# A gated cross-attention block on one core: the first two batches in another order, and part of the ternary weights on GpSimd

## What is computed

```python
x = x + tanh(g_xattn) * attention(layernorm(x), ctx, ctx)
x = x + tanh(g_ffn) * ffn(layernorm(x))

def attention(query, key, value):
    qk = einsum('bhqd,bhkd->bhqk', Q, K)               # Q, K, V: 512x512 linear layers with bias
    scores = qk / sqrt(32)
    feats = [scores.mean(), scores.max(-1).mean(), var(softmax(scores)).mean()]   # per batch and head
    t = exp(clip(mlp(feats), log 0.1, log 10))
    return linear(softmax(qk / (2 * t)) @ V, Wo, bo)

def ffn(x):                                            # 512 -> 2048 -> 512
    return bitlinear(gelu(bitlinear(x, w1)), w2)

def quant_weight(w):                                   # inside bitlinear
    s = clip(mean(abs(w)), 1e-5, None)
    return clip(round(w / s), -1, 1) * s               # ternary
```

## Time and profile before

| | us |
|---|---|
| median of 3 runs | 1429.16 (1427.7 to 1429.87) |
| profiled execution | 1428.32 |
| its span | 1426.5 |
| busy in the span: TensorE (matmul) | 1208.2 (85%) |
| VectorE | 1124.8 (79%) |
| ScalarE | 921.8 (65%) |
| GpSimd | 396.9 (28%) |
| mean granted TensorE clock, of full speed | 0.933 |

### The profile page before, as it was taken

The page is one execution under the profiler, slowest core; times in us unless marked ns, Lnnn a source line. Parts: engine busy times, 40 slices in busy tenths (PEclk is TensorE's granted clock), DMA queues, the critical chain, the costliest instruction groups (busy, mean ns, idle before and its releaser), DMA issues.

```text
span 1426.5 us, 23442 instructions
## 1 busy us (share of the span) xinstructions
PE 1208.2 (85%) x6684; PEld 445.5 (31%) x6684; DVE 1124.8 (79%) x2057; ACT 921.8 (65%) x1527; POOL 396.9 (28%) x369
## 2 busy tenths in 40 slices
PE   3624678998999999998999899999989899869958
PEld 1200231144313442244314341244214331223224
DVE  7189966988698878988698869988798879993246
ACT  2445458956597549856795649855895669645803
POOL 5354412531155102531145104520253101100210
PEclk9755688999999999999999999999999999889979
DMA  8241113011210122012301121012302110001000
GB/s 313 74 148 45 23 40 101 16 45 45 84 37 21 27 69 83 16 45 46 104 16 45 33 65 55 16 46 53 97 16 46 45 60 1 1 0 60 1 0 30
DMA packets 35315, 73.70 MB, mean 52 GB/s; under 512 B 7792, under 2 KB 7792, under 8 KB 34672
## 3 DMA queue, kind: packets, MB, share of 16 engines
q1 hardware_dynamic: 35184, 72.10, 17.6%
HBM read 38.39 MB, written 8.39 MB: 33 GB/s over the span
## 4 chain that ended last, share of the span: by engine, by line
PE 51%; DVE 26%; ACT 10%; issue 9%; POOL 2%; DVEq 1%; DMA 1%; SPq 1%; ACTq 1%; POOLq 0%
PE b_ps L1193 11%; DVE stat L868 7%; ACT region L712 5%; PE o_ps L1375 5%; PE o_ps L1193 5%; DVE nmax L863 5%; PE z_ps L1193 5%; PE a_ps L1214 4%; PE o_ps L1233 4%; PE b_ps L1220 3%; ACT etile L695 3%; PE b_ps L1354 2%; PE z_ps L1375 2%; PE b_ps L1365 2%; PE z_ps L1244 2%
## 5 line engine op out<-in xcount | busy, mean ns | idle before, releaser
L695 ACT ACTIVATE etile<-a_ps,nmax 128x512 f32<-128x512 f32 x512 | 371.3, 737 | 148.6 <-DVE nmax L863 148.4
L863 DVE TENSOR_REDUCE nmax<-a_ps 128x1 f32<-128x512 f32 x512 | 346.6, 678 | 68.8 <-PE a_ps L1214 65.1
L712 ACT ACTIVATE region<-b_ps,inv2t 128x512 f32<-128x512 f32 x512 | 355.0, 763 | 55.3 <-PE b_ps L1220 32.3
L868 DVE BATCH_NORM_STATS2 stat<-etile 128x6 f32<-128x512 f32 x512 | 348.3, 683 | 6.3 <-ACT etile L695 6.0
L1214 PE MATMUL a_ps<-kst,qst 96*128 96x512 f16 x512 | 206.0, 406 | 65.1 <-ACT etile L695 41.0
L1220 PE MATMUL b_ps<-qst,kst 97*128 97x512 f16 x512 | 194.5, 390 | 24.2 <-ACT region L712 15.9
L636 POOL TENSOR_TENSOR region<-region 128x512 f16<-128x512 f32 x64 | 81.0, 1268 | 240.2 <-ACT region L747 240.1
L1233 PE MATMUL o_ps<-region,vbuf 128*32 128x512 f32 x1024 | 138.1, 612 | 8.2 <-ACT region L712 6.3
L1244 PE MATMUL z_ps<-region,ones 128*32 128x512 f32 x1024 | 136.2, 604 | 9.5 <-DVE region L887 9.5
L1220 PEld LDWEIGHTS b_ps<-qst,kst 97*128 97x128 f16 x512 | 49.2, 96 | 301.3 <-ACT region L712 280.4
L571 POOL TENSOR_TENSOR region<-region 128x512 f32<-128x512 f32 x32 | 40.9, 1279 | 288.7 <-DVE region L894 288.7
(11 more groups left out here) (273 smaller groups left out, 1981.8 us busy)
## 6 DMA issues: line engine op xcount, KB each, us to landing
kst<-region SPq DMA_DIRECT2D x96, 128.0 KB, 2.3
qst<-region SPq DMA_DIRECT2D x96, 128.0 KB, 2.3
xres<-in_x_dram SPq DMA_DIRECT2D x8, 1024.0 KB, 5.3
out_dram<-xres SPq DMA_DIRECT2D x32, 256.0 KB, 2.1
cin<-in_ctxT_dram SPq DMA_DIRECT2D x30, 256.0 KB, 5.2
cin<-in_x_dram SPq DMA_DIRECT2D x28, 256.0 KB, 2.6
kst<-in_f1T_dram SPq DMA_DIRECT2D x2, 1024.0 KB, 11.5
qst<-in_f2T_dram SPq DMA_DIRECT2D x2, 1024.0 KB, 5.4
```

Source lines behind the costliest of these rows:

```text
L695: nc.scalar.activation(etile[:, k % E_SLOTS, :], a_ps[k % A_BANKS][:, :], ACT.Exp, bias=nmax[:, slot_of(n), t:t + 1], scale=1.0).then_inc( ...
L712: nc.scalar.activation(probs[:, s % 2, g, :], b_ps[g % 2][:, :], ACT.Exp, scale=inv2t[:, slot:slot + 1]).then_inc(b_exp, 1)
L863: vec.tensor_reduce(nmax[:, slot_of(k // T), k % T:k % T + 1], a_ps[k % A_BANKS][:, :], AX.X, ALU.max, negate=True).then_inc(a_max, 1)
L868: vec.bn_stats(stat[:, slot_of(k // T) * T + k % T, :], etile[:, k % E_SLOTS, :]).then_inc(a_stat, 1)
```

## The change

In body(-1), Q's weights are loaded and split before V's, the Q products stand right behind the turning of x, and V comes last; between the second and third V product TensorE waits for both stacks and then puts two scores ahead of each of the last two V products (`A_HEAD`, 4 tiles of batch 0). The biases are made by VectorE, not GpSimd. The two rows of ones are transfers, no memsets. ScalarE sums the magnitudes of chunks 0 and 1 behind Q's copies out and of the other six in body(0) (`MAGNITUDES_AT`); the tanh of the gates stands behind V.

In body(0), both scales and all eight ternary chunks are made: five by VectorE (`TERNARY_AT`, the set behind which each stands), three by GpSimd in quarters of 512 columns with three instructions each (chunks 0 and 1 between the splits of c, chunk 7 behind the last split of Q). The plan of batch 0's tiles is 28 in the sets and 36 in the products, three in each of K, V and Q. V stands in front of the turning of x. `stat_x` of the two pairs moves from behind sets 8 and 13 to the K stage, behind its first and third dense group, and GpSimd's normalising of a pair behind the splits of two K. In all bodies the load of the residual stands behind those of x.

The diff, cut to its core:

```diff
+A_PLAN_0 = (28, (3, 3, 3, 3, 0, 0, 0, 0, 3, 3, 3, 3, 3, 3, 3, 3))
+A_HEAD = 4
...
+MAGNITUDES_AT = {0: 2, 1: 3, 2: 6, 3: 4, 5: 5, 9: 7}
+SCALES_AT = {4: 0, 11: 1}
+TERNARY_AT = {5: 2, 7: 3, 13: 6, 14: 4, 15: 5}
+POOL_CHUNKS, DVE_CHUNKS = (0, 1, 7), (2, 3, 6, 4, 5)
...
+                    if isinstance(b, int) and b <= 1 and first == 0:
+                        sp_waits.wait_ge(bias_step, 1)
+                        sp.dma_start(kst[par][SHIFT:SHIFT + 1, :, :].rearrange("o h n -> o (h n)"),
+                                     ones16[0:H * T, :]).then_inc(kst_ones, 16)
...
                 if isinstance(i, int) and i == 0:
-                    sp_waits.wait_ge(w_lo_done, 4)
+                    for n in (2, 3, 4):
+                        load_f(n)
+                    load_c(1, 0)
+                    load_c(1, 1)
                     load_f(5)
-                    for n in (6, 7):
-                        sp_waits.wait_ge(f_tern, n - 3)
-                        load_f(n)
+                    load_f(7)
+                    load_c(1, 2)
+                    load_c(1, 3)
+                elif has_p and not first:
+                    for c in range(C):
+                        load_c(i + 1, c)
+                if has_p and not first:
+                    for n in range(T):
+                        load_x(i + 1, n)
                 if has_b:
+                    sp_waits.wait_ge(tern_pool, 3)
                     load_res(i - 1)
-                if has_p and not (isinstance(i, int) and i == -1):
-                    for c in range(2):
-                        load_c(i + 1, c)
                 if has_p:
...
-            load_w("v", WvT)
             load_w("q", WqT)
-            load_w("o", WoT)
             sp.dma_start(bias_row[:, 0, :], bv.partition_broadcast(P)).then_inc(bias_in, 16)
             sp.dma_start(bias_row[:, 1, :], bo.partition_broadcast(P)).then_inc(bias_in, 16)
+            load_w("v", WvT)
+            load_w("o", WoT)
...
-            pool.memset(kst[0][SHIFT:SHIFT + 1, :, :], 1.0).then_inc(kst_ones, 1)
-            pool_waits.wait_ge(kst_ones, 1)
...
+            def make_ternary(n):
+                k, w = n // 4, f_from[n]
+                dst = f1[:, n, :] if n < 4 else f2[:, 4 * (n - 4):4 * (n - 3), :].rearrange("p k n -> p (k n)")
+                high = above[n // 4]
+                pool_waits.wait_ge(f_sum, 2 * k + 2)
+                if n == 7:
+                    pool_waits.wait_ge(kst_in, 2 * 16 * 3 * G4)
+                for m in range(4):
+                    part = slice(m * S, (m + 1) * S)
+                    step = 3 * (4 * POOL_CHUNKS.index(n) + m)
+                    if step > 0:
+                        pool_waits.wait_ge(tern_step, step)
+                    pool.tensor_scalar(high, w[:, part], whalf[:, 1, k:k + 1], None, ALU.is_gt).then_inc(tern_step, 1)
+                    pool_waits.wait_ge(tern_step, step + 1)
+                    pool.tensor_scalar(w[:, part], w[:, part], whalf[:, 0, k:k + 1], None, ALU.is_lt) \
+                        .then_inc(tern_step, 1)
+                    pool_waits.wait_ge(tern_step, step + 2)
+                    pool.tensor_tensor(dst[:, part], high, w[:, part], ALU.subtract, saturate=False).then_inc(tern_step, 1)
+                pool_waits.wait_ge(tern_step, step + 3)
+                pool.sem_inc(tern_pool, 1)
...
+                if second:
+                    bank_n, before = mm_use(-1, "V", T - 1)
+                    pool_waits.wait_ge(mm_full[bank_n], before + 1)
+                if has_p and not first:
+                    for c in range(C):
+                        split_c(i + 1, c)
+                        if second and c % 2 == 1:
+                            make_ternary(c // 2)
...
                     inverse_deviation(0, mv1, mv1_done, var1_eps, rstd1, rstd1_done, parts=2, part=1, inc=2)
+                    split_qk(0)
+                    split_qk(1)
...
                 for n in range(C):
-                    if has_p:
+                    if has_p and not (first and n < 2):
                         split_qk(n)
+                    if second and n % 2 == 1:
+                        normalise_x(1, n // 2, from_cin)
+                        split_x(1, n - 1, from_cin)
+                        split_x(1, n, from_cin)
                     if has_b and n == 1:
...
+                if second:
+                    make_ternary(7)
...
+                if has_p and not second:
+                    x_out()
...
+                if first:
+                    magnitudes(0)
+                    magnitudes(1)
+                    v_out()
+                    act_waits.wait_ge(small_in, SMALL_LOADS)
+                    nc.scalar.activation(tg[:, :], gates[:, :], ACT.Tanh).then_inc(setup_tanh, 1)
...
             weight_lo(0, "k")
             stat_first_x()
-            weight_lo(1, "v")
+            weight_lo(1, "q")
...
+            weight_lo(2, "v")
+            weight_lo(3, "o")
...
+                    if second and s in SCALES_AT:
+                        ternary_scale(SCALES_AT[s])
+                    if second and s in TERNARY_AT:
+                        make_ternary(TERNARY_AT[s])
...
+                    if second and n % 2 == 0:
+                        stat_x(1, n // 2)
...
+                places = {len(pairs) * (n + 1) // (len(tiles) + 1): tile for n, tile in enumerate(tiles)}
...
+                def v_products():
+                    for t in range(T):
+                        rows = slice(t * P, (t + 1) * P)
+                        if first and t >= 2:
+                            if t == 2:
+                                pe_waits.wait_ge(qst_in, 16 * 3 * G4)
+                                pe_waits.wait_ge(kst_in, 16 * 3 * G4)
+                            score_a(0, 0, 2 * t - 4)
+                            score_a(0, 0, 2 * t - 3)
+                        if has_p:
+                            split_product(take(i, "V", t), [lambda c, x=x: x(c, rows) for x in c_parts],
+                                          [lambda c, w=w: w["v"][:, c, :] for w in (w_hi, w_lo)], tiles_a(C + T + t),
+                                          bias=0)
+                        else:
+                            alone(tiles_a(C + T + t))
...
+                if has_p and not second:
+                    turned_x()
...
+                        pe_waits.wait_ge(w_lo_done, 3)
+                        pe_waits.wait_ge(bias_step, BIAS_STEPS)
+                        v_products()
```

More of the change, by code:

```diff
@@ L1082, in body @@
                 has_a, has_b, has_p = stages(i)
+                second = isinstance(i, int) and i == 0
                 for s in range(SETS):
@@ L1249, in body @@
                 has_a, has_b, has_p = stages(i)
+                first, second = (isinstance(i, int) and i == n for n in (-1, 0))
                 if has_a:
@@ L1278, in alone @@
                         tile()
-                first = isinstance(i, int) and i == -1
                 if has_p:
```

248 lines of the change are left out of this document (115 added, 133 removed).

## The result

The changed kernel takes **1405.21 us** (median of 4 runs, 1404.38 to 1407.15), the kernel before 1429.51 (4 runs, 1427.7 to 1429.92): a ratio of 0.9832, 95% interval 0.9819 to 0.9844, 24.3 us less. The forecast was 1409.0 within 1402 to 1419, on the side of faster. The profiled execution took 1404.38 us, with a span of 1402.2 and a mean granted clock of 0.939.

What follows compares the result with a forecast made beforehand. VectorE was taken to bound the stretch from first score to value pass; the head 30.8 us shorter, the stretch 10.8 longer, so 1428.3 - 20.0 = 1408.3, median 1409, within 1402 to 1419 (the forecast's own range 1404 to 1414).

Steps and rivals of the forecast that it cites:

- The head: Set-up before the first exponential: it would start at 67.0 instead of 97.78 us, a gain of 30.8 us.
- Part (a): Head: without the GpSimd one-row memset VectorE's first cast takes 0.5, K products start 5.3 us earlier, at 13.9.
- (b): Head: Q no longer waits for V, so Q starts at 31.8 and its four products end at 44.0 us.
- (c): Head: Q's last copy out and split follow at once; Q stack issued at 46.5 instead of 83.5 us.
- Part (d): Head: four scores and V's last two products follow the stack wait, until 64.3; first exponential at 67.0 us.
- The set stage: From the first exponential to the K stage's first tile: 60.2 us on VectorE, ending at 127.2.
- the price of a VectorE ternary chunk: Set stage: five chunks on VectorE at 4.9 us each, 24.5 in all, bounds 18.0 and 26.5.
- The rival with 3.6 a chunk and half the wait: VectorE chunks cost 3.6 each and the wait for x half: 6.5 to 9 us better, 1402; chance 0.12.
- The K, V and X stages: From the K stage's first tile to the second Q stack: 62.6 us, so that stack is issued at 189.8.
- The new wait: K stage: VectorE stands 9.6 us for the load of x's second pair, lower bound 4, upper 14.
- the turn of x: Between the last V tile and score 52, behind V's last copy out and four copies of x: VectorE idles 4.0 us.
- The slower rival: TensorE stays at half clock in the K, V and Q stages and bounds eight products: +23.7, 1433 us; chance 0.03.

Runs made afterwards that it cites:

- e3: The changed kernel with GpSimd's one-row memset of 6.9 us back at the start: 1411.64 us, ratio 0.9869.
- e7: The changed kernel with no score tiles before the last two V products (A_HEAD = 0, their wait for the first stacks gone too): 1402.34 us, ratio 0.9805.
- e6: The changed kernel with GpSimd's three ternary chunks not computed, each a memset to zero (output differs): 1404.22 us, ratio 0.9818.
- e1: The changed kernel with the statistics of batch 1's second pair of x moved from the K stage to behind the V stage's second group: 1398.86 us, ratio 0.978.
- e5: e1 with three of the Q stage's twelve score tiles put between the second and third transposed tile of x: 1395.88 us, ratio 0.9757.
- e2: The changed kernel with the old plan of 40 tiles in the sets for batch 0: 1415.32 us, ratio 0.9895.

## Why the prediction was right, and by how much it missed

**The head** (30.8 forecast, 32.5 found: 97.78 - 65.26). Part (a), the cast, held: 0.43 for my 0.5, and e3 shows by itself that the memset was the cause. Its upper bound of +5 for a late load is off the table. Part (b) and (c) held within 1.0 us (45.47 for 46.5). Part (d) held in its result (65.26 for 67.0), but I priced the four early scores as neutral and never asked what the head would be without them; e7 shows that they cost about 3 us. The load of FFN chunk 2 was hidden here, as I had said; without the scores it ends last (a wait of 3.47 in e7).

**The set stage** (60.2 forecast, 55.0 found). **The step that failed is the price of a VectorE ternary chunk**: 4.9 taken, 4.03 measured, 4.3 us over five. I took a value near the disturbed row (5.3), where GpSimd was subtracting f32 tiles without a pause; the pairs now stand beside chunks and splits of c and take 3.62 to 4.64, and two of the five ran as if alone. Which of GpSimd's instructions disturbs least, no run separates. e6 puts the whole disturbance at 1.6 us. The rival with 3.6 a chunk and half the wait was the nearer one in this term and wrong in the other. What is left, 0.9 us, is mostly two tile statistics (0.6 each), which run two tiles late and so fall into the K stage: the stage has 51 maxima and statistics on VectorE where I had counted 53.

**The K, V and X stages** (62.6 forecast, 62.2 found). The new wait 9.56 for 9.6, the turn of x 3.96 for 4.0; e1 takes the first away and gains 6.35 for it, e5 half of the second. Here the chain of the prediction (split of K 1, normalising, splits, load) was followed step by step to the landing, and it held. Elsewhere two errors cancel: there are 74 maxima and statistics, not 72 (1.2 more), and from the last of them to the stack it is 1.6 us, where I had put 3.2 with a slow start of TensorE that this profile doesn't have. e2 confirms the term with which a thin V stage idles 1.73 per product.

**GpSimd.** A chunk costs 18.2 undisturbed, 17.0 taken; the two with what disturbs them 50.6 for 49.6. One compare is 1.57. The bias row gave 1.40 and was the right one; the normalising row, 2.07, has two operations. The Trainium skill (GPSIMD Engine Reference, Engine selection) has one-input work at roughly line rate and only two-input work at about half of it. The rows of this kernel disagree for the compare, 1.57 for 512 columns, where VectorE takes 1.27 for 2048; they come near it for the cast with one input (0.61 on GpSimd, 0.42 on VectorE) and the subtraction with two (1.16 and 0.69). That cost nothing here: e6 moved the first split of K by 2.0 us and nothing behind it. But a chunk up to 21 was not free, as the prediction has it: with 1.95 us left before the split of K 1, each of the two chunks could have taken about 1 us more. Chunk 7 ran from 182.44 to 200.65 into the value pass at no cost that shows: from the first issue of `mrow` to the next it is 140.2 in the changed kernel and 140.3 in e6, which doesn't compute it.

**The clock.** The slower rival needed TensorE at half clock through the dense stages. The mean was 0.87 from 120.3 to 182.5: it fell to 0.50 in the wait for x, where TensorE idles from 134.6 to 144.95, and stayed there to about 149; from 150 to 180 it was 1.00. So the rival did not come. What did come, in six other profiles, is one short stretch at 0.50 behind the turn of x, worth about 1.5 us (e6). The Trainium skill (TensorE: Matmul & The Clock Gate, A second HAM failure mode) tells of short idles that make the clock swing between its two levels; for the dense stages the trace speaks against a swing that repeats, and the last stretch shows a single one in seven of 13 profiles, for 2.0 us.

**The range.** The low end of 1402 rested on cheaper chunks together with half the wait for x; most of the first came and nothing of the second, so 1405.2 lies in the forecast's own range of 1404 to 1414, near its lower end. That rival was summed wrongly: its terms are 6.5 and 4.8, together 11.3, hence 1398 and outside the range; e1, with no wait for x at all, is at 1398.9. And the time is nearer to the forecast than the working is: the joint came 7.3 us earlier than I had put it (182.53 for 189.8), the time 3.8, because 2.0 in the last stretch and 1 us more were given back behind the joint. That is luck.

## What to carry to other kernels

When a load or a buffer moves later, write out its chain from the step that frees the buffer to the landing, and put the consumer in the engine's queue behind it: here the consumer stood 9.6 us in front of its data, and moving it alone gave 6.35 us (7.1 in distance). Work on an engine with time to spare pays by what it takes off the full one: 65 us of GpSimd for 10 us of VectorE. A piece of work put early into a wait is only free if nothing behind it is wanted: four scores in the head cost 3 to 4 us. And compare one profile with another piece by piece, from a joint of the same profile, with the granted clock beside each piece: here one stretch at half clock came and went by 2.0 us.

## What the runs showed that I had not expected

- A memset of one partition, 8192 f16 elements, takes 6.92 us on GpSimd, and holds a VectorE cast to f16 at 5.80 instead of 0.43.
- VectorE's and GpSimd's disturbance is mutual and uneven. Beside each other the compare of VectorE goes from 1.27 to 1.45 or 1.98, the pair's second step from 2.35 to 2.65, GpSimd's compares from 1.57 to 2.2 to 2.6 and its subtraction from 1.16 to 2.2 or 2.86. GpSimd carries most of it: its two chunks took 46.8 us instead of 36.4, VectorE's five pairs 20.15 instead of 18.54.
- The same program puts its first stack at 45.47, 46.50 or 46.21. The matmuls of the first K product stand 0.43 apart, the spacing of half clock, until 16.5, 17.6 and 17.4 (the windows view reads 1.00 there all the same), and Q's first product comes at 30.87, 31.61 and 31.39; the last 0.2 to 0.3 us arise behind it and are not explained.
- The same last stretch takes 142.1 or 144.1 us, by the granted clock: 0.72 or 1.00 in the same 6 us. One profile can't tell 2 us.
